# A three-phase image kernel: the order between its turns by the statistics, eight buffers for the first turn, and plain loads with VectorE's sum in the last

## The chip, the cores and the metric

One Trainium2 chip, one core. The time is the device time in microseconds of one execution of the whole program. TensorE (PE) multiplies matrices, VectorE (DVE) and ScalarE (ACT) work elementwise, GpSimd (POOL) does elementwise sums and issues some transfers, SyncE (SP) issues most transfers. Everything is float32.

## The reference

`x` is 8 images of 128 x 128 pixels and 256 channels. Two layers follow each other, each on a group-normalized copy with a residual:

```
x = x + L0(gn(x), gamma)           # v = gn(x) as (pixels, 256)
    aTa  = v^T v                   # 256 x 256, a Gram matrix over the whole image
    L0   = gamma * v softmax(aTa) + v
x = x + L1(gn(x), ...)
    x    = (x - min) / (max - min + eps)          # over the whole image
    m_k  = box sums of x over k x k, k = 2, 4, 8, 16
    alphas = slope of log m_k over log k          # per pixel and channel
    excite = sigmoid(relu(mean(alphas) w1 + b1) w2 + b2)
    sim    = cosine of log m_k and the fitted line
    L1     = sim * sigmoid(bn(alphas)) + (1 - sim) * x * excite
```

Three things are known only when a whole image has been read: the Gram matrix (and with it the mixing matrix and both group norms), the minimum and maximum of the layer's input, and `excite`.

## The kernel before

An image is cut into 16 chunks of 8 rows, a chunk into two units (two halves of 4 rows in the input, two halves of 128 channels behind it). Four stages work on four images at once, one image apart: **A** reads x and adds up the Gram matrix on TensorE (`gram_rows`, L498). **B** reads x again, turns it, multiplies it by the mixing matrix, adds the shift on VectorE and stores h to a scratch in HBM. **C** reads h back, makes the box sums (row pairs on VectorE, wider row sums t4 and t8 on GpSimd, sums over columns by band matrices on TensorE), takes logarithms and forms two arrays p and q, where the output is p + q * scale + offset; p and q go to scratch. **D** reads q, scales it (`scale_q`, L735), adds p, turns it back on TensorE (`turn_back`, L557), copies it out of PSUM (`copy_out`, L784) and stores it.

`images` (L222) runs eleven turns: turns 0, 1 and 2 fill up (A; A and B; A, B and C), turns 3 to 7 have all four stages, and turns 8, 9 and 10 drain (B, C, D; C, D; D alone). Each engine has its own program; a turn is eight pairs of chunks, and what must wait for a whole image stands between the turns, in an order written out by hand for each engine.

**Turn 0** loads x into `xa`, two buffers of 4 rows (512 KB each): SyncE loads a buffer once TensorE has used it (L266).

**Between the turns** VectorE does, in this order (L1130 to L1180): `value_range` (min and max, through a GpSimd reduction over partitions), `stats_columns` (ends with the diagonals for TensorE), `first_pairs` for both halves of the channels (the first chunk's row pairs of the next image), the squares and `norm` of stage C's last unit, `second_pairs` of half 0, `stats_logits`, `stats_step`, the last unit's `gated` product, `second_pairs` of half 1, then the means, products, moments and roots up to `stats_mix`. The `second_pairs` wait for GpSimd's first t4 sums, because the upper rows of t2 and t4 are zero pads that GpSimd clears with two memsets (L441, L442). GpSimd does `sum_p` of half 0, `first_sums` of half 0, `sum_p` of half 1, `first_sums` of half 1; `sum_p` is a DMA that adds one array to another in SBUF and waits for `tail_done`, which `gated` sets. ScalarE does the last unit's squares, then `guess_root`, then sigmoid and `invert`, then the softmax. TensorE stands still but for the small products of the statistics; its first box sum (`box` with which = 0) comes in the next turn, behind `rows1` (L684), the clearing matmuls (L606) and four rows of the Gram matrix.

**Turn 10** has stage D alone. For each unit SyncE loads q into one of four buffers, ScalarE scales it, and GpSimd adds p from HBM by an accumulating DMA:

```
def add_p(unit, at):
    pool.wait_ge(q_scaled, unit + 1)
    apart()
    g.dma_start(qd[:, at, :], p_dram[unit], accum_op=ALU.add).then_inc(sum_ready[at], 16)
```

Of the kernel before, what the change touches and what calls it, by code (L numbers as in the profile page):

```python
# [17 lines left out]
ROWS = 8  # L18
# [26 lines left out]
POOL_CONST = 10 + 1 + 2 * len(SCALES) + 2  # L45
POOL_PAIR, POOL_IMAGE = 4, 34
# [35 lines left out]
def mk_conv_preact(nc, x, gamma, w1, b1, w2, b2, bn_gamma, bn_beta, bn_mean, bn_var, out):  # L82
    with ExitStack() as ctx:
# [53 lines left out]

        def cols(at, n=2):
            return col[:, at:at + n]
# [28 lines left out]
        xa_used = sem("xa_used")  # L168
        xt_filled = sem("xt_filled")
# [64 lines left out]
        def _(sp):  # L234
# [77 lines left out]

            def turn(s, A, Bs, Cs, Ds):
                if (A or Bs):
                    loads(s, 0, 0, 0, A, Bs, False)
                if Ds:
                    for hf in range(2):
                        store_pq(32 * (s - 2) - 2 + hf, 16 * (s - 2) - 1, hf)
                    for p in pq_stored:
                        sp.wait_ge(p, 32 * CHUNKS * (s - 2))  # L320
                        apart()
                    loads(s, 0, 0, 0, False, False, True)
# [37 lines left out]
        def _(pool):  # L360
# [5 lines left out]
            g.memset(xa[:, :, :, C:C + 1], 1.0).then_inc(pool_const, 1)  # L366
            for j, value in enumerate((EPS, TINY, 1.0, GN_EPS)):
                g.memset(cst[:, j:j + 1], value).then_inc(pool_const, 1)
            g.memset(mx[:, :], -HUGE).then_inc(pool_const, 1)
            pool.wait_ge(pool_const, 10)  # L370
            made = 10
# [27 lines left out]
            def add_rows(dst, src, hf, k, gap):  # L399

                a = k * ROWS
                if k == 1:
# [10 lines left out]
            def more_row_sums(k, hf, count, pairs):  # L413

                pool.wait_ge(pool_done, own.now())
                pool.wait_ge(t_ready[2], pairs)
                add_rows(t4, t2, hf, k, 2)
                pool.wait_ge(pool_done, own.now())
                pool.wait_ge(t_ready[4], count)
                add_rows(t8, t4, hf, k, 4)  # L420
# [13 lines left out]
            def first_sums(image, hf, behind):  # L434

                if hf == 0:
                    if behind:

                        pool.wait_ge(log_ready[3], 32 * image)
                        apart()  # L440
                    g.memset(t2[:, :, ROWS - 2:ROWS, :], 0.0).then_inc(pool_done, own.one())  # L441
                    g.memset(t4[:, :, ROWS - 4:ROWS, :], 0.0).then_inc(pool_done, own.one())  # L442
                for m in range(2):
                    if m == 1:

                        pool.wait_ge(t_ready[8], 34 * image + 2 * hf + 1)
                        apart()
                    more_row_sums(1 - m, hf, 34 * image + 2 * hf + m + 1, 34 * image + 2 * m + hf + 1)

            def turn(s, A, Bs, Cs, Ds):  # L450
                image = s - 2
                def half_chunk(i, k, hf):
# [3 lines left out]
                    more_row_sums(1 - k if hf == 1 else k, 1 - hf, u + 4 + 2 * image, u + 4 + 2 * image)  # L456

                def pair(i, first, last):
                    for k in range(2):
                        for hf in range(2):  # L460
# [4 lines left out]
                            if Ds:  # L465
# [24 lines left out]
        def _(pe):  # L490
# [7 lines left out]
            def gram_rows(n, hf, half):  # L498
                if half == 0:
                    pe.wait_ge(xa_loaded[hf], 16 * (n + 1))  # L500
                for r in (2 * half, 2 * half + 1):
                    xr = xa[:, hf, r, :]
# [3 lines left out]
                if half == 1:  # L506
# [23 lines left out]
            def box(unit, k, hf, which, first):  # L530

                pe.wait_ge(t_ready[SCALES[min(which, 2)]], unit + (2 if first and which else 3) + 2 * image_of[0])
# [24 lines left out]
            def turn_back(unit, i, at, d):  # L557

                if d == 0:
# [7 lines left out]
            def half_chunk(s, i, k, hf, A, Bs, Cs, Ds, first):  # L567
# [7 lines left out]
                if Cs:  # L575
                    box(u, k, hf, 0, first)
                if Bs:
                    turn_x(nb, 2 * hf)
                if Cs:
                    box(u, k, hf, 2, first)  # L580
                    box(u, k, hf, 1, first)
                if Cs:
                    box(u, k, hf, 3, first)
# [5 lines left out]
                if Ds and not first:  # L589
                    turn_back(2 * nd + hf - 1, *behind(8 * (s - 3) + i, k, hf), 0)  # L590
# [821 lines left out]
```

## Time and profile before

| | us |
|---|---|
| median of 3 runs | 6241.43 (6239.41 to 6245.17) |
| the profiled execution | 6245.49, its span 6243.6 |
| DVE busy | 5222.7 (84% of the span) |
| PE busy | 4976.2 (80%) |
| ACT busy | 4828.5 (77%) |
| POOL busy | 1806.9 (29%) |

Row of the page: the span in 40 equal slices (156 us each), busy tenths of the engine in each slice (9 is 90% or more), and the granted TensorE clock in tenths of full speed.

```profile
PE   6968888699969998699969998799968887666632
DVE  1348999799979999799979999799989999788820
POOL 0012332233332333233323333333323332333311
PEclk9989999899989999899979999899979998788855
DMA  3544655588968988588858888589857777566678
```

How the rows further down are read. A line of the windows is: stretch in us from the start, its length, then busy us and instructions of PE, PE's weight loads, DVE, ACT and POOL, then the granted clock, the share of time that the 16 DMA engines were busy, and GB/s. A line of the waits is: engine, tile and line, what it waited for, us in total, times, longest. A line of the timeline is: start in us, us that it took, engine, line, operation, written and read tiles, shape, and how many of its kind in a row; in brackets the idle time ahead of it and what ended that. A line of the queues is: queue, packets, MB, share of the 16 engines' time. The turns end near 124, 419, 1092, 1790, 2490, 3190, 3890, 4590, 5293, 5976 and 6243 us.

### The profile page before, as it was taken

What the parts mean: (1) busy time and instruction counts of PE and PEld (TensorE: products, weight loads), DVE (VectorE), ACT (ScalarE), POOL (GpSimd) and SP (SyncE); (2) the same over time, 40 slices, a digit from 0 to 9 for tenths busy, and PEclk for the clock granted to TensorE, in tenths of its full rate; (3) what the DMA queues carried; (4) which work ended last, traced back from release to release, by engine and by line L of the source; (5) the groups of instructions that cost most, each with busy time, mean ns of one, the idle gap of its engine ahead of it and who ended that gap; (6) DMA issues with size and microseconds to landing.
All of it is one profiled execution on the core that took longest, in us unless ns stands there. A gap on an engine that the chain in (4) does not pass through costs nothing.

```text
span 6243.6 us, 108779 instructions
## 1 busy us (share of the span) xinstructions
PE 4976.2 (80%) x35320; PEld 4609.1 (74%) x35320; DVE 5222.7 (84%) x6293; ACT 4828.5 (77%) x5203; POOL 1806.9 (29%) x1361
## 2 busy tenths in 40 slices
PE   6968888699969998699969998799968887666632
PEld 5758888688858888688858887688857777566621
DVE  1348999799979999799979999799989999788820
ACT  0117888599959999599959999599959998688843
POOL 0012332233332333233323333333323332333311
PEclk9989999899989999899979999899979998788855
DMA  3544655588968988588858888589857777566678
GB/s 122 179 157 149 191 189 176 160 267 267 268 175 239 270 268 248 165 269 268 268 161 247 268 269 249 162 267 269 269 158 230 230 237 226 146 183 188 181 182 202
DMA packets 874514, 1344.68 MB, mean 215 GB/s; under 512 B 38704, under 2 KB 694096, under 8 KB 857936
## 3 DMA queue, kind: packets, MB, share of 16 engines
q1 hardware_dynamic: 800592, 1073.93, 49.1%
q0 software_dynamic: 73728, 268.47, 23.7%
q8 instruction: 85, 1.39, 0.1%
q14 instruction: 109, 0.89, 0.0%
HBM read 671.16 MB, written 536.87 MB: 193 GB/s over the span
## 4 chain that ended last, share of the span: by engine, by line
PE 36%; ACT 27%; issue 17%; DVE 10%; DMA 9%; ACTq 1%; POOL 1%; DVEq 0%; SPq 0%; POOLq 0%
PE even L545 14%; PE h_ps L526 8%; ACT logs L725 4%; ACT logs L763 4%; PE g_ps L503 4%; ACT logs L750 3%; ACT odd L725 3%; ACT logs L753 3%; DMA ut<-logs 3%; PE odd L554 3%; ACT logs L749 2%; DMA qd<-p_scratch 2%; PE o_ps L563 2%; ACT xt L712 2%; DMA hr<-h_scratch 2%
## 5 line engine op out<-in xcount | busy, mean ns | idle before, releaser
L545 PE MATMUL even<-band,t 128*128 128x128 f32 x12288 | 1871.0, 284 | 277.3 <-ACT logs L725 275.9
L545 PEld LDWEIGHTS even<-band,t 128*128 128x128 f32 x12288 | 1638.2, 199 | 330.5 <-issue 330.5
L407 POOL TENSOR_TENSOR t<-t 128x1024 f32<-128x1024 f32 (+3 forms) x800 | 1353.2, 1704 | 1034.1 <-DVE logs L1045 902.8
L526 PE MATMUL h_ps<-mix,xt 128*128 128x256 f32 x4096 | 994.1, 385 | 192.4 <-ACT xt L712 190.0
L526 PEld LDWEIGHTS h_ps<-mix,xt 128*128 128x128 f32 x4096 | 737.5, 190 | 322.4 <-ACT xt L712 242.0
L432 POOL DMA_DIRECT2D ut<-logs x256 | 224.6, 877 | 2588.4 <-DVE logs L1061 2508.4
L725 ACT ACTIVATE logs<-even,col 128x1024 f32<-128x1024 f32 x512 | 570.6, 1114 | 403.7 <-PE even L545 393.8
L547 PE MATMUL even<-band,t 128*128 128x128 f32 x4096 | 792.2, 275 | 0.0
L503 PE MATMUL g_ps<-xa 128*128 128x257 f32 x2048 | 621.9, 385 | 23.7 <-DMA xa<-in_x_dram 23.7
L563 PE MATMUL o_ps<-ident,qd 128*128 128x128 f32 x2048 | 359.2, 304 | 349.1 <-ACT o_sb L790 205.1
L930 DVE CUSTOM_DVE_ANT_0 h_out<-h_ps,shift,mx 128x512 f32<-128x512 f32 x512 | 383.0, 748 | 293.5 <-PE h_ps L526 289.6
L547 PEld LDWEIGHTS even<-band,t 128*128 128x128 f32 x4096 | 622.4, 192 | 0.0
L563 PEld LDWEIGHTS o_ps<-ident,qd 128*128 128x128 f32 x2048 | 269.6, 155 | 404.6 <-ACT o_sb L790 231.2
L545 PE MATMUL odd<-band,t 128*128 128x128 f32 x4096 | 516.0, 281 | 4.3 <-ACT ut L732 4.3
L545 PEld LDWEIGHTS odd<-band,t 128*128 128x128 f32 x4096 | 496.6, 198 | 4.6 <-issue 4.6
L712 ACT ACTIVATE xt<-xt_ps 128x512 f32<-128x512 f32 x512 | 300.3, 586 | 230.3 <-PE xt_ps L516 230.3
L504 PEld LDWEIGHTS g_ps<-xa 128*128 128x128 f32 x2048 | 390.7, 191 | 58.2
L961 DVE SCALAR_TENSOR_TENSOR t<-hr,col 128x128 f32<-128x128 f32 (+1 forms) x368 | 358.9, 975 | 73.2 <-POOL t L407 36.3
L790 ACT ACTIVATE o_sb<-o_ps 128x512 f32<-128x512 f32 x512 | 299.1, 584 | 127.6 <-PE o_ps L563 126.9
L1007 DVE TENSOR_TENSOR logs<-logs 128x1024 f32<-128x1024 f32 x256 | 388.5, 1517 | 10.4 <-DMA ut<-logs 8.2
L504 PE MATMUL g_ps<-xa 128*128 128x129 f32 x2048 | 396.0, 275 | 0.0
L739 ACT ACTIVATE qd<-qd,col 128x1024 f32<-128x1024 f32 x256 | 315.4, 1232 | 78.1 <-DMA qd<-q_scratch 56.4
(185 smaller groups left out, 10100.0 us busy)
## 6 DMA issues: line engine op xcount, KB each, us to landing
xa<-in_x_dram SPq DMA_DIRECT2D x256, 512.0 KB, 8.6
xb<-in_x_dram SPq DMA_DIRECT2D x256, 512.0 KB, 8.5
h_scratch<-h_out SPq DMA_DIRECT2D x128, 1024.0 KB, 8.7
hr<-h_scratch SPq DMA_DIRECT2D x256, 512.0 KB, 6.8
q_scratch<-logs SPq DMA_DIRECT2D x256, 512.0 KB, 4.6
ut<-logs POOLq DMA_DIRECT2D x256, 512.0 KB, 6.5
p_scratch<-ut SPq DMA_DIRECT2D x256, 512.0 KB, 2.6
qd<-q_scratch SPq DMA_DIRECT2D x256, 512.0 KB, 8.3
```

What stands on the lines that cost most here:

```text
L407: ins = g.tensor_tensor(dst[:, hf, d:d + n, :], src[:, hf, d:d + n, :], src[:, hf, e:e + n, :], ALU.add)
L503: t.matmul(g_ps[:, 0:C + 1], xr[:, 0:CH], xr[:, :], start=False, stop=False, skip_group_check=True)
L504: ins = t.matmul(g_ps[:, C + 1:C + 2 + CH], xr[:, CH:C], xr[:, CH:C + 1], start=False, stop=False, skip_group_check=True)
L526: ins = t.matmul(h_ps[:, r * C:(r + 1) * C], xt[:, q % 2, jh, r, :], mix[:, jh, :], start=(jh == 0), stop=(jh == 1))
L545: ins = t.matmul(o, src[:, hf, at, :], band[:, which, :], start=True, stop=(which < 3))
L547: ins = t.matmul(o, t8[:, hf, new + j, :], band[:, which, :], start=False, stop=True)
L563: ins = t.transpose(o_ps[:, r * CH:(r + 1) * CH], qd[:, at, (4 * d + r) * W:(4 * d + r + 1) * W], ident[:, :])
L712: a.activation(xt[:, q % 2, :, :, :].rearrange("p j r w -> p (j r w)"), xt_ps[:, :], ACT.Copy).then_inc(xt_copied, 1)
L725: a.activation(dst, src[:, :], ACT.Ln, bias=col[:, EPSR:EPSR + 1]).then_inc(log_ready[which], 1)
L930: d.tensor_tensor_reduce(h_out[:, k, 2 * q:2 * q + 2, :].rearrange("p r c -> p (r c)"), h_ps[:, :], shift[:, :, :].rearrange("p r c -> p ( ...
L961: ins = d.scalar_tensor_tensor(t2[:, hf, at:at + rows, :], hr[:, hf, at:at + rows, :], col[:, NEG2:NEG2 + 1], hr[:, hf, before:before + ro ...
L1007: d.tensor_tensor(logs[:, hf, 4, :], logs[:, hf, 0, :], logs[:, hf, 2, :], ALU.add).then_inc(dve_done, own.one())
```

## The change

**Turn 0.** `first_turn` of SyncE loads x into eight buffers in turn: the two of `xa` and six that lie in t2 and t4, which nothing uses in this turn. `first_grams` of TensorE works through them in a loop of four times eight. GpSimd writes ones into the six new buffers' last column.

**Turn 10.** `last_turn` of SyncE loads q and p of each unit with plain transfers, p into `late_p`, which lies in t8, and then stores the chunk two back. `add_p` of VectorE adds them after ScalarE has scaled q. GpSimd has nothing to do in this turn.

**Between the turns.** VectorE: `stats_columns` goes ahead of everything, `value_range` and the squares follow, then `stats_logits`, `norm`, `stats_step`, then the first row pairs of both halves in one piece, and then the last unit's product. `second_pairs` and its wait for GpSimd are gone. GpSimd: both `sum_p` come ahead of both `first_sums`; the memsets of t2 and t4 are gone, and the sums over the upper rows copy 2 rows (4 for t8) and add 6 (4) where they added 8 rows. ScalarE: `guess_root` goes ahead of the squares, the softmax ahead of `invert`. TensorE: the first box sum of the next turn goes between the moments and `rows1`.

```diff
+            def first_turn():
+
+                def eight(g, first):
+                    for j in range(8):
+                        if not first:
+                            sp.wait_ge(xa_used, 8 * g + j - 5)
+                            apart()
+                        sp.dma_start(early[j][:, :, 0:C], x_sub[8 * g + j]).then_inc(early_loaded[j], 16)
+                eight(0, True)
+                with sp.Fori(1, 4) as g:
+                    eight(g, False)
+
+            def last_turn(s):
+
+                def pair(i, first):
+                    for k in range(2):
+                        nd = 16 * (s - 3) + 2 * i + k
+                        for hf in range(2):
+                            at = 2 * k + hf
+                            sp.wait_ge(o_filled, 2 * (2 * nd + hf) + 2)
+                            apart()
+                            sp.dma_start(qd[:, at, :], q_dram[2 * nd + hf]).then_inc(q_loaded[at], 16)
+                            sp.dma_start(late_p[:, at, :], p_dram[2 * nd + hf]).then_inc(p_loaded[at], 16)
+                        if not first:
+                            store(nd - 2, k)
+
+                def store(nd, k):
+                    sp.wait_ge(o_copied, 4 * nd + 5)
+                    apart()
+                    sp.dma_start(out_chunk[nd], o_sb[:, k, :, :]).then_inc(o_stored[k], 16)
+                pair(0, True)
+                with sp.Fori(1, PAIRS) as i:
+                    pair(i, False)
+                for k in range(2):
+                    store(16 * (s - 2) - 2 + k, k)
...
-            def first_sums(image, hf, behind):
-
-                if hf == 0:
-                    if behind:
-
-                        pool.wait_ge(log_ready[3], 32 * image)
-                        apart()
-                    g.memset(t2[:, :, ROWS - 2:ROWS, :], 0.0).then_inc(pool_done, own.one())
-                    g.memset(t4[:, :, ROWS - 4:ROWS, :], 0.0).then_inc(pool_done, own.one())
+            def first_sums(image, hf):
+
                 for m in range(2):
-                    if m == 1:
-
-                        pool.wait_ge(t_ready[8], 34 * image + 2 * hf + 1)
-                        apart()
-                    more_row_sums(1 - m, hf, 34 * image + 2 * hf + m + 1, 34 * image + 2 * m + hf + 1)
...
+                if top:
+                    apart()
+                    g.tensor_copy(dst[:, hf, a:a + gap, :], src[:, hf, a:a + gap, :]).then_inc(pool_done, own.one())
+                    parts = [(a + gap, a, ROWS - gap)]
+                elif k == 1:
...
-                    sum_p(32 * (s - 1) - 2, 0)
-                if Bs:
-                    first_sums(s - 1, 0, Cs)
-                if Cs:
-                    sum_p(32 * (s - 1) - 1, 1)
-                if Bs:
-                    first_sums(s - 1, 1, False)
+                    for hf in range(2):
+                        sum_p(32 * (s - 1) - 2 + hf, hf)
+                if Bs:
+
+                    for hf in range(2):
+                        first_sums(s - 1, hf)
 
             images(lambda lo, hi: own.loop(lo, hi, POOL_IMAGE), turn)
...
+            def first_grams():
+                with pe.Fori(0, 4) as g:
+                    for j in range(8):
+                        pe.wait_ge(early_loaded[j], 16 * (g + 1))
+                        gram_of(early[j], range(SUB), True)
+
...
+                if d == 0 and alone:
+                    pe.wait_ge(p_added, unit - 2 * CHUNKS * (B - 1) + 1)
+                elif d == 0:
                     pe.wait_ge(sum_ready[at], 16 * (i + 1))
...
+                if Bs:
+
+                    box(32 * (s - 1), s - 1, 0, 0, 0, True)
+                if A:
+                    stats_rows(s)
...
                     offset(u - 1, 16 * (s - 1) - 1, 1)
+                if A:
+                    guess_root(s, var_ready, VAR, RS, rs_guess)
+                if Cs:
                     square_contrasts(u - 1, 16 * (s - 1) - 1, 1, (0, 1))
-                if A:
-                    guess_root(s, var_ready, VAR, RS, rs_guess)
-                if Cs:
                     sigmoid(u - 1, 1, (0, 1, 2))
+                if A:
+                    softmax_exp(s)
+                if Cs:
                     invert(u - 1, 1, (0, 1, 2, 3))
-                if A:
-                    softmax_exp(s)
                 if Cs:
...
+                row_pairs(1, hf, load, False)
...
+            def add_p(unit, i, at):
+                dve.wait_ge(q_scaled, unit + 1)
+                dve.wait_ge(p_loaded[at], 16 * (i + 1))
+                d.tensor_tensor(qd[:, at, :], qd[:, at, :], late_p[:, at, :], ALU.add).then_inc(p_added, 1)
...
+                if A:
+                    stats_columns(s)
...
-                if A:
-                    stats_columns(s)
-                if Bs:
-                    first_pairs(s - 1, 0)
-                    first_pairs(s - 1, 1)
                 if Cs:
                     two = two_squares(u - 1, 1)
                     add_slopes(u - 1, 1)
                     three = three_squares(u - 1, 1, two)
+                if A:
+                    stats_logits(s)
+                if Cs:
                     norm(u - 1, 1, three)
-                if Bs:
-                    second_pairs(s - 1, 0)
-                if A:
-                    stats_logits(s)
+                if A:
                     stats_step(s, Bs)
+                if Bs:
+                    for hf in range(2):
+                        first_pairs(s - 1, hf)
                 if Cs:
                     gated(u - 1, 1, product(u - 1, 1, similarity(u - 1, 1)))
-                if Bs:
-                    second_pairs(s - 1, 1)
```

## Rows read from the trace of the kernel before

**Rows 1.** Windows over turn 0, one boundary and turn 10.
```profile
10.00:124.00 114.00, 90.74 (x510) 80.06 (x510) 0.00 (x0) 0.00 (x0) 0.00 (x0) 0.99 0.45 140
2490.00:2553.00 63.00, 16.64 (x61) 14.16 (x61) 50.51 (x111) 15.92 (x23) 23.89 (x17) 0.53 0.49 151
6008.00:6243.00 235.00, 71.33 (x256) 45.84 (x256) 0.00 (x0) 73.66 (x94) 25.89 (x30) 0.50 0.82 202
```

**Rows 2.** Waits of TensorE in turn 0, 10 to 124 us.
```profile
PE g_ps L503 <- DMA xa<-in_x_dram: 23.3, 15, 1.9
```

**Rows 3.** Timeline of the boundary between turns 4 and 5.
```profile
2496.11 1.23 DVE L1061 SCALAR_TENSOR_TENSOR logs<-logs,ut 128x1024 f32<-128x1024 f32 x1
2498.09 2.39 DVE L1200 TENSOR_SCALAR col<-col 128x2 f32<-128x2 f32 x1
2499.19 1.26 POOL L442 MEMSET t<- 128x1024 f32 x1
2500.92 0.16 DVE L1271 TENSOR_SCALAR col<-col 128x2 f32<-128x2 f32 x1
2503.82 0.28 DVE L1282 TENSOR_SCALAR h_out<-ones,col 128x128 f32<-128x128 f32 x1
2529.52 1.22 DVE L1049 TENSOR_TENSOR logs<-logs 128x1024 f32<-128x1024 f32 x1
2534.67 5.23 POOL L407 TENSOR_TENSOR t<-t 128x1024 f32<-128x1024 f32 x2
2543.79 0.42 DVE L1348 TENSOR_TENSOR h_out<-h_out,o_ps 128x256 f32<-128x256 f32 x1
2550.97 2.07 PE L684 MATMUL o_ps<-h_out,ones 128*128 128x128 f32 x8 [3.38 <-DVE h_out L1369]
2562.60 2.02 PE L545 MATMUL even<-band,t 128*128 128x128 f32 x16 [0.94 <-ACT logs L725]
```

**Rows 4.** Timeline, boundary of turns 8 and 9: a small VectorE operation beside GpSimd's sums.
```profile
5331.30 5.12 POOL L407 TENSOR_TENSOR t<-t 128x256 f32<-128x256 f32 x4 [1.09 <-DVE t L961]
5335.45 0.98 DVE L1230 SCALAR_TENSOR_TENSOR col<-col,late 128x2 f32<-128x2 f32 x1
```

**Rows 5.** Timeline, boundary of turns 0 and 1: VectorE's logits and step.
```profile
134.73 0.69 DVE L1286 COPY h_out<-xt_ps 128x512 f32<-128x512 f32 x1 [2.83 <-PE h_ps L653]
144.10 0.48 DVE L1333 SCALAR_TENSOR_TENSOR h_out<-h_out,col,xt 128x256 f32<-128x256 f32 x1
```

**Rows 6.** Timeline, boundary of turns 1 and 2: one `row_pairs`.
```profile
458.51 1.53 DVE L961 SCALAR_TENSOR_TENSOR t<-hr,col 128x128 f32<-128x128 f32 x2
```

**Rows 7.** Timeline, boundary of turns 8 and 9: last `norm`, second box.
```profile
5309.39 1.23 DVE L1045 TENSOR_TENSOR logs<-logs 128x1024 f32<-128x1024 f32 x1
5339.05 3.75 PE L545 MATMUL even<-band,t 128*128 128x128 f32 x16 [2.30 <-ACT logs L725]
```

**Rows 8.** Timeline of turn 10: beginning, two output copies, last store.
```profile
5989.50 0.86 POOL L432 DMA_DIRECT2D ut<-logs  x1 [11.48 <-DVE logs L1061]
5997.27 1.77 SPq L278 DMA_DIRECT2D qd<-q_scratch  x4
6000.75 2.44 ACT L739 ACTIVATE qd<-qd,col 128x1024 f32<-128x1024 f32 x2 [9.34 <-DMA qd<-q_scratch]
6058.64 0.60 ACT L790 ACTIVATE o_sb<-o_ps 128x512 f32<-128x512 f32 x1 [4.20 <-PE o_ps L563]
6062.33 0.60 ACT L790 ACTIVATE o_sb<-o_ps 128x512 f32<-128x512 f32 x1 [0.16 <-PE o_ps L563]
6238.85 0.40 SPq L351 DMA_DIRECT2D out_dram<-o_sb  x1
```

**Rows 9.** DMA queues in turn 10, 6040 to 6230 us.
```profile
q1 hardware_dynamic: 16727, 25.98, 44.9%
q0 software_dynamic: 3698, 13.44, 39.3%
```

**Rows 10.** DMA queue of SyncE in turn 9, 5400 to 5900 us.
```profile
q1 hardware_dynamic: 49437, 65.57, 36.6%
```

More of the change, by code:

```diff
@@ L168, in mk_conv_preact @@
         xa_used = sem("xa_used")
+        early_loaded = [sem(f"early_loaded{j}") for j in range(8)]
+        p_loaded = [sem(f"p_loaded{j}") for j in range(4)]
+        p_added = sem("p_added")
         xt_filled = sem("xt_filled")
@@ L366, in _ @@
             g.memset(xa[:, :, :, C:C + 1], 1.0).then_inc(pool_const, 1)
+            for j in range(2, 8):
+                g.memset(early[j][:, :, C:C + 1], 1.0).then_inc(pool_const, 1)
             for j, value in enumerate((EPS, TINY, 1.0, GN_EPS)):
@@ L499, in gram_rows, with gram_of @@
                 if half == 0:
[L500 to L502 removed]
+                    pe.wait_ge(xa_loaded[hf], 16 * (n - CHUNKS + 1))
+                gram_of(xa[:, hf, :, :], (2 * half, 2 * half + 1), half == 1)
+            def first_grams():
[3 more added lines that the diff above has]
+                        gram_of(early[j], range(SUB), True)
+            def gram_of(x, rows, last):
+                for r in rows:
+                    xr = x[:, r, :]
                     t.matmul(g_ps[:, 0:C + 1], xr[:, 0:CH], xr[:, :], start=False, stop=False, skip_group_check=True)
@@ L505, in gram_rows @@
                                    skip_group_check=True)
-                if half == 1:
+                if last:
                     ins.then_inc(xa_used, 1)
@@ L528, in mix_x, with box @@
                 ins.then_inc(h_filled, 1)
-            def box(unit, k, hf, which, first):
-                pe.wait_ge(t_ready[SCALES[min(which, 2)]], unit + (2 if first and which else 3) + 2 * image_of[0])
+            def box(unit, image, k, hf, which, first):
+                pe.wait_ge(t_ready[SCALES[min(which, 2)]], unit + (2 if first else 3) + 2 * image)
                 if which == 0:
@@ L574, in half_chunk @@
                     gram_rows(n, hf, 0)
-                if Cs:
-                    box(u, k, hf, 0, first)
+                if Cs and not first:
+                    box(u, image_of[0], k, hf, 0, first)
                 if Bs:
@@ L589, in half_chunk @@
                 if Ds and not first:
-                    turn_back(2 * nd + hf - 1, *behind(8 * (s - 3) + i, k, hf), 0)
+                    turn_back(2 * nd + hf - 1, *behind(8 * (s - 3) + i, k, hf), 0, not Cs)
                 if A:
@@ L595, in half_chunk @@
                 if Ds and not first:
-                    turn_back(2 * nd + hf - 1, *behind(8 * (s - 3) + i, k, hf), 1)
+                    turn_back(2 * nd + hf - 1, *behind(8 * (s - 3) + i, k, hf), 1, not Cs)
             image_of = [None]
@@ L610, in pair @@
                             half_chunk(s, i, k, hf, A, Bs, Cs, Ds, first and k == 0 and hf == 0)
-                pair(0, True)
-                with pe.Fori(1, PAIRS) as i:
-                    pair(i, False)
+                if not (Bs or Ds):
+                    first_grams()
+                else:
+                    pair(0, True)
+                    with pe.Fori(1, PAIRS) as i:
+                        pair(i, False)
                 if Cs:
@@ L1069, in half_chunk @@
                 v, vf = u - 1, 1 - hf
+                if Ds and not Cs:
+                    add_p(2 * nd + hf, i, 2 * k + hf)
                 if tail:
```

55 lines of the change are left out of this document (31 added, 24 removed).

## Prediction

> **What bounds the kernel now.** I read the slices first. In most of the span VectorE is 90% busy or more; dips come at the two ends and between the turns, and the change touches only these. So I priced three stretches, with the windows, then the waits, then the timeline. In turn 0 TensorE is busy 90.7 of 114 us, and what it lacks it waited for one thing, the load of x, 23.3 us in 15 waits [rows 1, 2]. At a boundary between full turns TensorE works 16.6 of 63 us, VectorE 50.5 [rows 1]: the reader should see a chain that runs through VectorE, with one end at `rows1` (L684) and the second box sum (L545) as the point where the next turn is under way [rows 3]. In turn 10 nobody is busy, but the DMA engines are at 0.82 [rows 1]: 44.9% of their time is the plain queue with 25.98 MB, 39.3% GpSimd's accumulating queue with only 13.44 MB [rows 9]. An accumulated byte costs 1.7 times a plain one.
>
> **Turn 0.** The gain is the wait for loads: with eight buffers a load has seven units of time to land, and TensorE's own work stays. At TensorE's pace (two units, each 512 KB, in 2 x 2.65 us: 90.7 us less 5 for start and clearing, over 32) the engines must move some 200 GB/s; they moved 140 at a share of 0.45 [rows 1], so that is a share of about 0.64, and they hold. **23.3 us** saved. Six small memsets come ahead on GpSimd, below 1 us together and beside the loads of the parameters: 0, or 1 without that cover.
>
> **A boundary between full turns.** I lay the new order along the old clock [rows 3]. The last `gated` of the loop ends at 2497.3. `stats_columns` comes now at once; it took from 2500.9 to 2504.0, 3.1 us. Then the rest of what stood from 2497.3 to 2500.9, 3.6 us, of which 2.2 was one tiny operation (L1200, 2.39 us, where its like take 0.16) that ended with GpSimd's memset; that memset is gone, so 1.4: 2501.8. Two squares sums and a slope sum, 1.2 + 0.2 + 1.2 (L1049's kind): 2504.4. Logits, softmax and step: 9.85 us where GpSimd is idle [rows 5], with `norm` inside ScalarE's softmax: 2514.3. TensorE's products for the logits (3 us after the diagonals) are under the squares. Row pairs: four steps of the size of the 1.53 us for one [rows 6], 6.0: 2520.3. Three operations of 1.2 to 1.25: the last product ends at T = 2524.0. Before, they began at 2529.5 and so ended at 2533.3 [rows 3].
>
> Now GpSimd. Its wait for `tail_done` stands ahead of all its sums; queued behind it are all sixteen of its operations, and TensorE's second box waits for them. In the old trace the sums began 1.4 us behind the product (2534.67 [rows 3]). One half took 5.2 + 5.1 us [rows 3, 4]; the new upper part copies 6 of its 16 rows instead of adding them, so I estimate 9 a half, 18 for both: GpSimd is busy from T + 1.4 to T + 19.4 = 2543.4. VectorE's statistics run beside it, and the trace shows what that costs: L1200 ended at 2500.48, the memset at 2500.45 [rows 3]; a 128x2 operation with two SBUF inputs (L1230, 0.98 us) ended at 5336.43, GpSimd's four sums at 5336.42 [rows 4]. A small VectorE operation of this kind waits for the end of GpSimd's current one. The chain from the moments to the diagonals has fourteen of them, GpSimd has sixteen; so I let the chain end with GpSimd's last sum, plus 0.8: `rows1` at 2544.2 instead of 2551.0, 6.8 us earlier. The rule has a name: the Trainium skill, "SBUF — State Buffer", Who interferes with whom, says that GpSimd and VectorE share one port pair as an exclusive lock, held for the whole instruction. It speaks against putting the sums beside the statistics, and the trace agrees (2.39 against 0.16 us).
>
> TensorE's box goes under this chain: sixteen matmuls of 2.0 us, and ScalarE's logarithm behind it, for which the second box waited 0.9 [rows 3]. Its new wait, for the row pairs of half 0, is over at 2517; `rows1` stands behind it, and the diagonals come last. 2.8 us more. Nothing else is late: `scale_q` needs q on the chip, 11.3 us after `sum_p` is issued (5989.5 to 6000.75 [rows 8]), so T + 12. Together **9.5 us**. The bounds: 0 (the chain comes as late as before) and 21.5 (GpSimd costs nothing). ScalarE's `guess_root` costs its squares 0.5 us, and they are not last.
>
> There are six such boundaries, and the one between turns 1 and 2 has the same statistics: 7 x 9.5. **Boundary 8 to 9** has none. `norm` ended at 5310.6 [rows 7]; it loses 2.2 of memset and 2.8 of row pairs ahead: 5305.6, then pairs 6.0 and products 3.7, 5315.3. q is there 0.6 + 11.3 later, 5327.2, scaling and logarithm 2.3, second box at 5329.5 for 5339.05: 9.5 again, with half 0's sums done at 5326. Sum of boundaries: **76 us**.
>
> **Turn 10.** A chunk moves 3.146 MB (q, p, out). The plain queue's rate is 25.98 MB in 0.449 x 190 us, 305 GB/s [rows 9]: 10.33 us a chunk with the engines always busy, 165.3 for 16. It starts at 5997.3 with 1.8 us of latency (3.5 to q's use, less 1.7 for its bytes [rows 8]). Behind the last load come scaling and the new sum, 1.2 each, 3.7 of turning and copying (one unit apart: 6058.64 to 6062.33), and of the last store's 4.75 us to the end of the span 1.35 that are not bytes: 7.5 [rows 8]. End at 6171.9 instead of 6243.6, **71.7 us**. The sum on VectorE, 1.2 of 5.2 us a unit, is hidden under the transfers; so are TensorE and ScalarE (3.7 a unit). New waits: TensorE on `p_added`, VectorE on p, and SyncE on the copies of a chunk with the next chunk's loads behind it. Bounds: at turn 9's rate, 358 GB/s [rows 10], 8.8 a chunk, gain 96.4; at the old share of busy time, 84%, 12.3 a chunk, gain 40.2. I take the turn's own rate, since its mix of packets is nearest. The Trainium skill, "DMA: Bandwidth & Descriptors", Where 436 GB/s comes from, gives some 358 GB/s as a core's share of HBM; by it the chunk would take 8.8 us and the sum would be 6046.
>
> **Sum.** 23.3 + 76 + 71.7 = 171.0. The profiled execution took 6245.5, so 6074.5; the median of the runs lies 4.1 below it, so **6070**.
>
> **The rivals.**
> (a) Turn 10 is held by its round trips, not by bytes: four buffers, a store queued behind loads, engines 84% busy as now. For it: they never were fuller in this turn. Against: the accumulation, which put GpSimd and a second landing into each round trip, is gone. 12.3 us a chunk: 6102.
> (b) GpSimd's sums cost the chain nothing, because VectorE gets in first. Then from L1348 to `rows1` pass 7.2 us as in the old trace [rows 3], from T + 1.0: 2532.2, 12.0 earlier than my 2544.2, seven times: 5986. Against: both stalls above.
> (c) The boundaries give nothing: VectorE and GpSimd hold each other up, and the second box comes as late as before. For it: in the old order the sums were spread over the gaps. 76 more: 6146.
> (d) Turn 0 doesn't do what it says: SyncE doesn't run ahead and TensorE waits as before. 23.3 more: 6094.
> (e) Slower: in turn 10 nothing overlaps, since SyncE stands at the store's wait with the loads behind it. Loads 6.9 + 1.8, scaling, sum and two units 9.8, store 4.75: 23.3 a chunk, 372.8 against the present 246.3, 126.5 more, less the 99.3 of the other two stretches: 27.2 more than now, 6269. It decides from 21.6 us a chunk, (246.3 + 99.3) / 16. Against: four buffers are loaded ahead of that wait.
>
> **How the numbers follow.** Forecast 0.54 (own range 6040 to 6102), (a) 0.20, (b) 0.09, (c) 0.09, (d) 0.06, (e) 0.02. The range is 6010 to 6110: it holds the forecast, (a) and (d), and leaves out (b), (c) and (e), 0.20. All but (e) and a mixture near it are faster: faster by over 0.2% 0.97, within 0.2% 0.01, slower 0.02 (0.2% is about what a measurement of this kernel can tell from no change).
>
> **What would show it.** Turn 0: no wait for x, its end near 101 us instead of 124. A boundary: `stats_columns` 3.4 us earlier, GpSimd's sums in one block of about 18 us, small VectorE operations of 0.5 to 1.8 us inside it, `rows1` right behind it. If these are 0.16 us, (b) holds. Turn 10: DMA share above 0.9 with 290 to 310 GB/s; a share near 0.84 is (a). The turns' own inside must not change; if it does, the sum is wrong by what they share.

## The result, and the profile after

| | before | after |
|---|---|---|
| median, us | 6243.3 (6239.41 to 6245.38) | 5991.08 (5982.8 to 5995.84) |
| ratio | | 0.9595 [0.9581, 0.9609] |
| span of the profiled execution, us | 6243.6 | 5992.4 |

The change takes 252 us off. The forecast was 6070; the kernel is 79 us faster than that and lies below the range of 6010 to 6110. The profiled spans differ by 251.2 us.

From the page of after: busy time of the engines, then the 40 slices (150 us each), to be laid beside the slices of before.

```profile
PE 4980.4 (83%) x35320; PEld 4617.6 (77%) x35320; DVE 5203.9 (87%) x6325; ACT 4822.4 (80%) x5203; POOL 1749.3 (29%) x1351
DVE  1349999899989999899998999899998999788882
DMA  4645555689967988698877898689876787566669
```

TensorE, VectorE and ScalarE do the same work within 20 us; only idle time went. The dips of VectorE between the turns are 8 where they were 7, and the last slice has the DMA engines at 9.

Where it went, from turn to turn. Turn 0 is measured to the end of its last matmul (124.5 us in before, 96.0 in after). A boundary is measured from the first operation of `range_columns` (L1184 in before, L1254 in after), which hands the range of the image to GpSimd and is called the start of the range below, to the second box sum (L545, L601), the point at which the next turn is under way.

| stretch | predicted | measured |
|---|---|---|
| turn 0 | -23.3 | -28.5 |
| eight boundaries | -76 | -124.5 |
| inside the turns | 0 | +3.8 |
| turn 10 (first load of q to the end of the span) | -71.7 | -102.0 |

| boundary of turns | 1/2 | 2/3 | 3/4 | 4/5 | 5/6 | 6/7 | 7/8 | 8/9 |
|---|---|---|---|---|---|---|---|---|
| before, us | 58.95 | 70.93 | 74.93 | 75.38 | 75.47 | 74.64 | 70.37 | 46.21 |
| after, us | 48.72 | 55.22 | 55.67 | 55.47 | 56.17 | 55.65 | 55.49 | 40.03 |

Windows of after that answer to [rows 1], with turn 0 cut a little wider; the first line is that same stretch of before.

```profile
9.00:119.00 110.00, 86.74 (x482) 75.78 (x481) 0.76 (x6) 0.00 (x0) 0.00 (x0) 0.98 0.46 143
9.00:91.00 82.00, 82.00 (x484) 74.33 (x484) 0.77 (x6) 0.00 (x0) 0.00 (x0) 1.00 0.63 198
5850.00:5990.00 140.00, 71.25 (x256) 45.75 (x256) 39.21 (x32) 74.38 (x96) 0.00 (x0) 0.50 0.98 354
```

In turn 0 TensorE does as many matmuls in 82 us as before in 110, without a gap. In turn 10 the DMA engines are at 0.98 and move 354 GB/s; they moved 202 [rows 1].

The boundary between turns 4 and 5 in after (timeline; it answers to [rows 3]). The range starts at 2415.0 here and at 2487.2 in before, so 72.2 is to be taken off the clock of before. Rows between those shown are left out.

```profile
2450.67 1.22 DVE L1126 SCALAR_TENSOR_TENSOR logs<-logs,ut 128x1024 f32<-128x1024 f32 x1
2452.51 0.86 POOL L490 DMA_DIRECT2D ut<-logs  x1 [25.38 <-DVE logs L1126]
2453.05 0.72 POOL L458 COPY t<-t 128x256 f32<-128x256 f32 x1
2456.46 3.76 PE L601 MATMUL even<-band,t 128*128 128x128 f32 x16
2456.83 0.16 DVE L1430 TENSOR_TENSOR col<-col 128x2 f32<-128x2 f32 x1
2458.86 0.87 DVE L1309 TENSOR_SCALAR h_out<-ident,col 128x128 f32<-128x128 f32 x4
2460.01 1.70 PE L752 MATMUL o_ps<-h_out,ones 128*128 128x128 f32 x8
2460.82 1.80 POOL L465 TENSOR_TENSOR t<-t 128x768 f32<-128x768 f32 x1 [7.05 <-issue]
2465.92 1.09 ACT L793 ACTIVATE logs<-even,col 128x1024 f32<-128x1024 f32 x1
2470.25 0.39 POOL L458 COPY t<-t 128x256 f32<-128x256 f32 x1
2470.43 1.80 PE L601 MATMUL even<-band,t 128*128 128x128 f32 x11 [2.14 <-POOL t L465]
```

The last product (L1126, the T of the prediction) ends at 2451.9, GpSimd's first copy comes 1.2 us later, as forecast. But then GpSimd does nothing for 7.05 us, released by nothing that the profile shows ("issue"). In this hole VectorE's small operations run at 0.16 us, and `rows1` (L752) begins at 2460.0, before GpSimd's first real sum. The second box waits for the sums of half 0, which end at 2470.3; the logarithm (L793) was done at 2467.0.

I had overlooked the same hole in the trace of before. Two of its rows that stand in no group above, the reduction over partitions and the first sums behind it:

```profile
2494.08 0.59 POOL L476 PARTITION_ALL_REDUCE rr<-rr  x1 [17.05 <-issue]
2507.80 4.88 POOL L407 TENSOR_TENSOR t<-t 128x1024 f32<-128x1024 f32 x2 [7.35 <-DVE t L976]
```

The row of 7.35 names VectorE's row pairs as its releaser, and those of half 0 were done at 2505.5, 2.3 us before the sums; that hid the hole. The memsets of [rows 3] stand between the reduction and it, and they ran without one.

The reduction itself starts late too. VectorE hands over its last input (L1189) at 2487.84, and the reduction starts at 2494.08, 6.2 us later; at all eight boundaries of both kernels this is 5.9 to 6.3 us. It costs next to nothing here, since VectorE comes to the result later than that or waits 0.2 us for it (8/9 of after).

### The profile page after: what moved, and what is told of

It reads as the page before. It is cut to its first block and busy times, and to the rows that moved or that the text cites. A ratio compares the mean times of both kernels' runs of the same rounds, so it can differ in the third digit from the quotient of the medians.

```text
span 5992.4 us, 108675 instructions
## 1 busy us (share of the span) xinstructions
PE 4980.4 (83%) x35320; PEld 4617.6 (77%) x35320; DVE 5203.9 (87%) x6325; ACT 4822.4 (80%) x5203; POOL 1749.3 (29%) x1351
## 5 line engine op out<-in xcount | busy, mean ns | idle before, releaser
L601 PE MATMUL even<-band,t 128*128 128x128 f32 x12288 | 1886.2, 285 | 304.5 <-ACT logs L793 266.6
L601 PEld LDWEIGHTS even<-band,t 128*128 128x128 f32 x12288 | 1652.0, 200 | 358.2 <-issue 336.6
L465 POOL TENSOR_TENSOR t<-t 128x1024 f32<-128x1024 f32 (+3 forms) x800 | 1315.7, 1657 | 876.1 <-DVE logs L1110 779.6
L793 ACT ACTIVATE logs<-even,col 128x1024 f32<-128x1024 f32 x512 | 569.8, 1113 | 380.6 <-PE even L601 370.6
L559 PE MATMUL g_ps<-xa 128*128 128x257 f32 x1856 | 561.7, 384 | 0.3 <-DMA xa<-in_x_dram 0.3
L601 PE MATMUL odd<-band,t 128*128 128x128 f32 x4096 | 515.0, 280 | 0.0
L601 PEld LDWEIGHTS odd<-band,t 128*128 128x128 f32 x4096 | 496.2, 198 | 0.0
L1072 DVE TENSOR_TENSOR logs<-logs 128x1024 f32<-128x1024 f32 x256 | 397.1, 1551 | 9.6 <-DMA ut<-logs 7.1
L560 PEld LDWEIGHTS g_ps<-xa 128*128 128x128 f32 x1856 | 354.4, 191 | 52.7
L1030 DVE SCALAR_TENSOR_TENSOR t<-hr,col 128x128 f32<-128x128 f32 (+1 forms) x368 | 334.6, 909 | 43.7 <-DMA hr<-h_scratch 38.8
L1105 DVE TENSOR_TENSOR logs<-logs 128x1024 f32<-128x1024 f32 x256 | 313.7, 1225 | 59.6 <-ACT logs L821 46.2
L560 PE MATMUL g_ps<-xa 128*128 128x129 f32 x1856 | 359.8, 276 | 0.0
```

Source lines behind the costliest of these rows:

```text
L465: ins = g.tensor_tensor(dst[:, hf, d:d + n, :], src[:, hf, d:d + n, :], src[:, hf, e:e + n, :], ALU.add)
L559: t.matmul(g_ps[:, 0:C + 1], xr[:, 0:CH], xr[:, :], start=False, stop=False, skip_group_check=True)
L560: ins = t.matmul(g_ps[:, C + 1:C + 2 + CH], xr[:, CH:C], xr[:, CH:C + 1], start=False, stop=False, skip_group_check=True)
L601: ins = t.matmul(o, src[:, hf, at, :], band[:, which, :], start=True, stop=(which < 3))
L793: a.activation(dst, src[:, :], ACT.Ln, bias=col[:, EPSR:EPSR + 1]).then_inc(log_ready[which], 1)
L1030: ins = d.scalar_tensor_tensor(t2[:, hf, at:at + rows, :], hr[:, hf, at:at + rows, :], col[:, NEG2:NEG2 + 1], hr[:, hf, before:before + ro ...
```

## Experiments

Two explanations are tried. Theory R: behind the reduction over partitions GpSimd's first elementwise sum pays some 7 us in which nothing runs, and this hole keeps its sums away from VectorE's chain. Rival L: VectorE's small operations hold GpSimd out until they are through.

### The order alone, and the ends alone

order_only is the changed kernel with turns 0 and 10 as before; ends_only is the kernel before with the new turns 0 and 10.

```diff
# order_only, from the changed kernel
-                if not (Bs or Ds):
-                    first_turn()
-                    return
...
-                    if not Cs:
-                        last_turn(s)
-                        return
...
-                            if Ds and Cs:
+                            if Ds:
                                 add_p(...)
...
```

> The new order between the turns alone; turn 0 and turn 10 are as before. If the boundaries gave what the two traces differ by there (second box 10 to 20 us earlier at eight boundaries, 124 us in all), the time is 6243 - 124 = 6119, between 6110 and 6130. If my sum of 76 us was right and the rest came from the ends or from inside the turns, it is 6167.

> Turn 0 and turn 10 new, the order between the turns as before. By the two traces the ends gave 28.7 and 101.9 us: 6243 - 131 = 6112, and with order_only the two savings add up to the whole 251 within 5 us. By my sum (23.3 and 71.7) it is 6148. If the parts need each other, the savings don't add up.

Measured: order_only 6128.32 us, ratio 0.9817 [0.9801, 0.9834], 114.8 us gained; ends_only 6107.01, ratio 0.9784 [0.9767, 0.98], 136.2 us gained. Together 251.0 for a whole of 252: the parts don't touch each other. Each lies up to 9 us off what the stretches of the two traces had let expect (6119 and 6112), in opposite directions. Both savings are above the forecast's 76 and 95.0. In order_only `rows1` of boundary 4/5 comes 44.97 us behind the start of the range, as in after.

### A tiny sum that takes the hole away, and no reduction at all

```diff
# warm, from the changed kernel
 g.partition_all_reduce(rr[:, 2:4], rr[:, 0:2], 128, RMAX).then_inc(range_out, 1)
+pool.wait_ge(pool_done, own.now())
+g.tensor_tensor(spare[:, :], cst[:, 0:2], cst[:, 2:4], ALU.add).then_inc(pool_done, own.one())
...
# no_reduce, from the changed kernel
-g.partition_all_reduce(rr[:, 2:4], rr[:, 0:2], 128, RMAX).then_inc(range_out, 1)
+g.tensor_copy(rr[:, 2:4], rr[:, 0:2]).then_inc(range_out, 1)
```

> The changed kernel with one more tiny sum (128x2) on GpSimd right behind the reduction over partitions. Theory R (the first elementwise sum of GpSimd behind a reduction starts 7 us late, because GpSimd changes its code; this gap kept its sums out of VectorE's statistics): the tiny sum takes the 7 us, GpSimd's first real sum follows its copy at once, 2 us behind the last product instead of 9; small VectorE operations then last 0.5 to 1.8 us, rows1 comes 6 to 12 us later than in the changed kernel at the seven boundaries with statistics, and the kernel is 15 to 60 us slower than it, 6005 to 6050. Theory L (VectorE's stream of small operations keeps GpSimd out until it ends): the gap stays where it is and the time stays at 5991.

> The changed kernel with the reduction over partitions replaced by a plain copy on GpSimd, so the range is that of each partition alone. Theory R: no gap of 7 us ahead of GpSimd's first sum at any boundary, and the same collision with VectorE's small operations as in warm. Theory L: the gap is still there.

Measured: warm 6021.1 us, ratio 0.9644 [0.9628, 0.966]; no_reduce 6021.84 in a single run. Timeline of warm at the boundary between turns 4 and 5 (the range starts at 2425.5):

```profile
2441.10 0.77 POOL L526 TENSOR_TENSOR spare<-cst 128x2 f32<-128x2 f32 x1 [7.74 <-issue]
2463.63 0.73 POOL L459 COPY t<-t 128x256 f32<-128x256 f32 x1
2464.00 2.13 POOL L466 TENSOR_TENSOR t<-t 128x768 f32<-128x768 f32 x1
2466.87 1.28 DVE L1295 TENSOR_SCALAR gate<-gate 128x2 f32<-128x2 f32 x1
2468.86 1.72 DVE L1435 TENSOR_TENSOR col<-col 128x2 f32<-128x2 f32 x1
2476.00 4.00 DVE L1312 TENSOR_SCALAR h_out<-ident,col 128x128 f32<-128x128 f32 x4
2480.24 2.07 PE L755 MATMUL o_ps<-h_out,ones 128*128 128x128 f32 x8 [9.86 <-DVE h_out L1442]
```

The tiny sum, which has no business but to be there, takes the 7.7 us, at a place where nobody needs GpSimd. The real sums then follow their copy at once, and they meet the chain: 1.28 us for 0.16, 1.72 for 0.16, 4.00 for four that took 0.87. `rows1` comes at 54.7 instead of 45.0. So a kernel without the hole is 30 us slower. And without the reduction, at the same boundary of no_reduce, there is no hole:

```profile
2431.11 0.18 POOL L523 COPY rr<-rr 128x2 f32<-128x2 f32 x1 [10.78 <-DVE mx L1259]
2468.73 2.12 POOL L465 TENSOR_TENSOR t<-t 128x768 f32<-128x768 f32 x1
```

Theory R holds: the hole belongs to the change from the reduction to elementwise sums, a copy does not pay it (the copy at 2453.05 in after stood ahead of it), and L falls, since in both runs the sums start amid the same small operations. A reduction that lasts longer than its row says is out as well: in after the hole comes 30 us behind the reduction, with DMA issues and a copy in between. In no_reduce the copy that stands for the reduction starts 0.2 us behind VectorE's last input, where the reduction took 6 us to start: the change to the reduction has its delay too. The Trainium skill, "GPSIMD Engine Reference", Instruction dispatch, says that GpSimd's kernels can be loaded at run time and that the first call to a freshly loaded one pays some 6 us with no visible instruction. The rows agree in kind, at 6.9 to 8.1 us, which is more; that the way back to the ordinary sums costs it too is this case's to show.

### The hole closed and the sums held back

```diff
# warm_hold, from warm
                 if Bs:
+                    if A:
+                        pool.wait_ge(diag1_ready, s + 1)
+                        apart()
                     for hf in range(2):
                         first_sums(s - 1, hf)
```

> The changed kernel with two additions: the tiny GpSimd sum (128x2) right behind the reduction over partitions, as in the run named warm, and at each boundary that has group-norm statistics GpSimd's first sums wait until the new diagonals are ready (diag1_ready), so they run behind VectorE's small operations and not beside them. Theory R (the first elementwise sum behind the reduction reloads GpSimd's code for 7 us, and this gap is what kept the sums out of the chain; beside the sums every small VectorE operation waits for GpSimd's current one): rows1 comes 45 us behind the start of the value range as in the changed kernel (54.7 in warm), the sums start at once behind the wait, half 0 is done some 9.5 us later, the second box starts at 54 to 55 (55.5 in the changed kernel, 63.5 in warm); boundary 8 to 9, which has no such wait, keeps warm's 36.3 (40.0 in the changed kernel). Sum 7 x 1 + 3.7: 5980 to 5988 us. Rival: the order between VectorE and GpSimd is not what delayed warm, the tiny operation or something it moves is: then 6010 to 6025 as warm.

> The run named warm_hold once more, beside the changed kernel on the same chip, to say whether it beats it. Expected from the first look and the sum 7 x 0.3 (second box 55.2 instead of 55.5) + 3.8 (boundary 8 to 9) + the boundary of turns 1 and 2 (43.25 instead of 48.7, 5.5): 8 to 11 us under the changed kernel, ratio to the kernel before 0.957 to 0.959. Rival: the difference of 8 us was one of the places: a ratio within 0.001 of the changed kernel's.

> The changed kernel itself, beside hold_again on the same chip: 5985 to 5997 us, ratio to the kernel before 0.958 to 0.961.

Measured: 5983.44 us, ratio 0.9577 [0.9561, 0.9593], and again 5982.06, 0.9584 [0.9571, 0.9597], beside the changed kernel's 5989.96, 0.9595 [0.9582, 0.9608]. Timeline of warm_hold, same boundary (the range starts at 2413.25):

```profile
2458.20 1.16 PE L757 MATMUL o_ps<-h_out,ones 128*128 128x128 f32 x8
2458.57 0.40 POOL L459 COPY t<-t 128x256 f32<-128x256 f32 x1 [6.94 <-DVE h_out L1444]
2458.94 1.80 POOL L466 TENSOR_TENSOR t<-t 128x768 f32<-128x768 f32 x1
2468.50 2.05 PE L606 MATMUL even<-band,t 128*128 128x128 f32 x16 [0.53 <-POOL t L466]
```

`rows1` is back at 45.0. Only a wait separates this kernel from warm, and it is 38 us faster: that is what keeping the sums off the chain is worth. `rows1` comes 9.7 us earlier at each full boundary; the second box, which waits for the later sums, comes 4.2 to 8.8 us earlier at the seven boundaries with statistics and 48 in all, of which about 10 are lost again inside the turns. The second box comes at 55.25 here (55.47 in after), at 43.25 for 48.72 at boundary 1/2, and at 36.27 for 40.03 at 8/9, where the hole stood on the path of after. Both medians lie some 8 us under the changed kernel's, with intervals that overlap: likely better, not proven so.

### The hole in the old order

```diff
# warm_before: the two lines of warm in the kernel before
```

> The kernel before with the same tiny GpSimd sum behind the reduction over partitions. Theory R: the reload now lies from about 2494.7 to 2501.7 of the old clock and is over when the first row pairs are ready (2505.5), so the first sums start at 2505.5 instead of 2507.8; the second row pairs come when VectorE reaches them (2514.9) and waited for nothing. What is gained is at most 2.3 us a boundary, and it is not on the chain: 6228 to 6245, so the reload that was overlooked in the old profile cost the old order next to nothing. Rival: the old order was held by the reload, 7 us at each of 8 boundaries: near 6190.

Measured: 6230.79 us, ratio 0.998 [0.997, 0.999]; 12 us gained, inside what was expected. GpSimd's timeline, boundary 4/5 (the range starts at 2479.3):

```profile
2494.78 0.63 POOL L479 TENSOR_TENSOR spare<-cst 128x2 f32<-128x2 f32 x1 [8.06 <-issue]
2498.02 5.61 POOL L408 TENSOR_TENSOR t<-t 128x1024 f32<-128x1024 f32 x2 [0.17 <-POOL t L443]
```

The sums start at 18.8 instead of 20.6, and `rows1` comes at 61.2 instead of 63.7. I had said that nothing of this is on the chain; 2.4 to 2.6 us were at each of the boundaries 2/3 and 4/5 to 7/8, and 1.0 at 3/4. The rival, 7 us each, is out.

### Turn 10

late_accum: the changed kernel with p added again by GpSimd's accumulating DMA, SyncE's order of loads and stores kept. late_gpsimd: p loaded plainly, but from GpSimd's queue. late_no_p: no load of p.

```diff
# all three: last_turn, from the changed kernel
-                            sp.dma_start(late_p[:, at, :], p_dram[2 * nd + hf]).then_inc(p_loaded[at], 16)
...
# late_accum
-                            if Ds and Cs:
+                            if Ds:
                                 add_p(u - 32, 2 * k + hf)
...
# late_gpsimd
+                            if Ds and not Cs:
+                                pool.wait_ge(o_filled, 2 * (u - 32) + 2)
...
+                                g.dma_start(late_p[:, 2 * k + hf, :], p_dram[u - 32]).then_inc(p_loaded[2 * k + hf], 16)
```

> The changed kernel, but in turn 10 p is added again by GpSimd's accumulating DMA (VectorE's sum and the plain load of p are gone), while SyncE keeps the new order of loads and stores. Theory A (the accumulating DMA's bytes are dear, some 12 us of the DMA engines' time a chunk against 8.5): turn 10 takes 200 to 246 us instead of 144.4, the DMA share 0.82 to 0.95 at 200 to 250 GB/s, so 6050 to 6093 us. Rival B (the order of loads and stores and the number of buffers set the old turn, the accumulation does not matter): turn 10 stays near 144, 5985 to 6000 us.

> The changed kernel, but in turn 10 the plain load of p is issued by GpSimd through its own queue, where it stood before, and VectorE sums. Theory A (only the accumulation is dear): the same as the changed kernel, 5985 to 6000 us, 340 to 354 GB/s. Rival C (GpSimd's software queue is slow, whatever it carries): p's packets there take 1.5 to 1.9 times as long, turn 10 takes 190 to 246 us, 6035 to 6093 us.

> The changed kernel without the load of p in turn 10: VectorE still adds, but an old content of the buffers, so this leaves p out of the last image's output. A chunk moves 2.1 MB instead of 3.15 MB. If turn 10 of the changed kernel is bound by bytes (0.98 of the engines' time, 8.6 us a chunk), the transfers need 5.9 us a chunk and something else becomes the bound: in the old trace two output copies lay 3.7 us apart, which is 7.4 us a chunk. Then turn 10 takes 16 x 7.4 + 8 = 126 us instead of 144.4 and the kernel 5973; if TensorE and ScalarE overlap better than that, down to 16 x 5.9 + 8 = 102, 5949. The DMA share falls below 0.85 in the first case and stays above 0.95 in the second. Rival: round trips or the issue order bound turn 10, not bytes: then leaving p out changes nothing, 5985 to 5995.

| | median, us | ratio | turn 10, us |
|---|---|---|---|
| changed kernel | 5991.08 | 0.9595 [0.9581, 0.9609] | 144.3 |
| late_accum | 6096.37 | 0.9763 [0.9747, 0.9779] | 241.6 |
| late_gpsimd | 5993.3 | 0.9595 [0.9579, 0.9611] | 138.5 |
| late_no_p | 5976.64 | 0.957 [0.9556, 0.9585] | 126.7 |

The times of turn 10 are those of one trace each, and they vary from execution to execution: the changed kernel took 144.3 us and, in after_again, 141.9; warm_hold 143.2 and, as hold_again, 134.8. The DMA engines are busy all the time in the shortest too, at a higher rate (window of hold_again):

```profile
5842.00:5972.00 130.00, 71.21 (x256) 45.69 (x256) 39.22 (x32) 74.42 (x96) 0.00 (x0) 0.50 1.00 380
```

So a difference of less than 10 us in this column says nothing by itself, that of late_gpsimd among them.

Queues over 120 us of turn 10 (5860 to 5980): first the changed kernel, then late_accum (q1 is SyncE's, q0 GpSimd's), then late_gpsimd.

```profile
q1 hardware_dynamic: 22614, 44.09, 101.6%
```

```profile
q1 hardware_dynamic: 10630, 16.80, 42.7%
q0 software_dynamic: 2416, 8.78, 40.8%
```

```profile
q1 hardware_dynamic: 17983, 29.89, 66.8%
q0 software_dynamic: 4365, 15.91, 34.1%
```

On GpSimd's queue a plain load runs at 15.91 MB in 0.341 x 120 us, 389 GB/s, and the accumulating one at 8.78 MB in 0.408 x 120 us, 179 GB/s. It is the accumulation that is dear, not the queue. The kernel came out 3 us above the 6050 to 6093 expected of theory A, with nothing left for B. The order of loads and stores gave next to nothing by itself: late_accum has the new one and takes 241.6 us, before took 246.3. In it the engines are at 0.82 and TensorE waits up to 17 us for p (windows and waits of late_accum):

```profile
5850.00:6080.00 230.00, 69.09 (x248) 44.41 (x248) 0.00 (x0) 73.28 (x94) 27.72 (x32) 0.50 0.82 213
PE o_ps L618 <- DMA qd<-p_scratch: 133.5, 17, 17.2
```

Without p the turn is 17.6 us shorter (the kernel 14), at a DMA share of 0.82 (window and waits of late_no_p), so then TensorE and ScalarE hand each other the two halves of a unit, (126.7 - 7.5) / 16 = 7.4 us a chunk, as expected from [rows 8]. The changed kernel is bound by bytes, but only 0.5 to 1.1 us a chunk above that next bound, by the spread of 134.8 to 144.3 us.

```profile
5860.00:5970.00 110.00, 67.51 (x243) 43.57 (x244) 37.20 (x31) 69.92 (x91) 0.00 (x0) 0.50 0.82 273
PE o_ps L620 <- ACT o_sb L857: 37.8, 54, 0.8
```

## Why the prediction was right or wrong

**What bounds the kernel.** Right: the change moved only the three kinds of stretch, and they gave 255.0 us, of which 3.8 came back inside the turns.

**Turn 0.** The mechanism was right: no wait of the matmuls is left, and 1.2 us of their weight loads; rival (d) is out. The size was low, 23.3 for 28.5. The step that failed is "TensorE's own work stays": over the same matmuls TensorE's busy time fell from 86.74 to 82.00 us. The row of its weight loads, which I passed over, has the whole wait; the matmuls' row [rows 2] starts counting only when the last matmul has run out (waits of before, 5 to 125 us; the matmuls' own row says 23.3 over this stretch as well):

```profile
PEld g_ps L503 <- DMA xa<-in_x_dram: 27.6, 16, 2.1
```

Another part is a stretch of before in which the granted clock was at its lower level, 1.2 GHz, behind a wait of 1.9 us for x; the 0.79 over 8 us is 3.4 us of it (window of before, then of after, then of order_only):

```profile
32.00:40.00 8.00, 7.19 (x32) 6.18 (x32) 0.00 (x0) 0.00 (x0) 0.00 (x0) 0.79 0.35 110
32.00:40.00 8.00, 8.00 (x52) 7.33 (x51) 0.00 (x0) 0.00 (x0) 0.00 (x0) 1.00 0.63 203
32.00:40.00 8.00, 6.41 (x37) 5.72 (x38) 0.00 (x0) 0.00 (x0) 0.00 (x0) 1.00 0.50 149
```

That part belongs to this one execution and not to the change: order_only and warm_before load x as before did, have no such stretch in turn 0, and end it at 122.1 and 123.0 us instead of 124.5, so beside them the gain is 26 to 27. The six memsets ahead cost nothing, as said.

**A boundary: VectorE's chain up to the product.** Right. `stats_columns` came 3.3 us earlier (3.4 forecast), and the product ended 36.9 us behind the start of the range (36.8 forecast).

**GpSimd beside it.** The step that failed: "In the old trace the sums began 1.4 us behind the product", which I carried over to the new order. Those sums were the second ones behind the reduction [rows 3]; the ones that move to T + 1.4 are now the first, and pay the hole. The sums started at T + 8.9. The contention that I priced is real and a little cheaper than I put it: in warm, where the hole is gone, `rows1` comes at T + 17.8, against my T + 20.2, and the second box 63 to 64 us behind the start of the range where all four stages run. In the changed kernel the chain slipped through the hole instead, 9.7 us earlier than in warm. It did so at six boundaries. At 1/2 the hole ends too soon, and there the contention that I forecast is in the changed kernel itself (timeline of after):

```profile
422.63 1.63 DVE L1430 TENSOR_TENSOR col<-col 128x2 f32<-128x2 f32 x1
431.24 3.00 DVE L1309 TENSOR_SCALAR h_out<-ident,col 128x128 f32<-128x128 f32 x4
```

`rows1` comes 42.2 us behind the start of the range there, and 33.1 in warm_hold.

**Rival (b)** gave `rows1` at 2532.2 on the old clock, 45.0 behind the start, and it was measured at 45.04, so its number for `rows1` was right. Its 5986 for the whole, near the 5991 measured, was luck: it had 160 us for the boundaries, 35.5 more than they gave, and turns 0 and 10 gave 35.5 more than it had for them. Its reason, that VectorE gets in first, was not: take the hole away and the stalls are there, and at 1/2 they are there with it. I gave it 0.09 because both stalls in the trace spoke against it, and they did; what was missing was the question when GpSimd could start.

**The second box.** I let it come 2.8 us sooner behind `rows1` than before, held by nothing else. It is held by half 0's sums (2.14 us in the row of after above), and comes 10.4 behind `rows1` where it was 11.6. So the boundaries gave 19 to 20 us each where all four stages run, 15.7 and 14.9 at 2/3 and 7/8, 10.2 at 1/2. **At 8/9** I said 9.5 and got 6.2: there the hole lies on the path (timeline of after).

```profile
5175.17 0.72 POOL L458 COPY t<-t 128x256 f32<-128x256 f32 x1
5182.83 1.79 POOL L465 TENSOR_TENSOR t<-t 128x768 f32<-128x768 f32 x1 [6.94 <-issue]
5191.74 3.73 PE L601 MATMUL even<-band,t 128*128 128x128 f32 x16 [12.13 <-POOL t L465]
```

Half 0's sums, which I had done at T + 11, ended at T + 18; warm, where they ran at once, gained the 3.75 us. In all the boundaries gave 48.5 more than forecast. Rival (c) is out.

**Turn 10.** The mechanism was right: engines always busy, the sum on VectorE hidden, the new waits free; rivals (a) and (e) are out. The term that was mis-sized is the rate, 10.33 us a chunk. It measured (144.3 - 7.5) / 16 = 8.6 us (8.0 in the shortest execution, 134.8), and the gain was 102.0 instead of 71.7, near my bound of 96.4 at turn 9's rate [rows 10]. I took the turn's own plain rate, 305 GB/s [rows 9], "since its mix of packets is nearest"; but that rate was taken beside the accumulating transfers, which the change removes. In late_accum SyncE's plain bytes go at 16.80 MB in 0.427 x 120 us, 328 GB/s; in late_gpsimd, where the same queue carries the same transfers and only the accumulation is gone, at 29.89 in 0.668 x 120, 373; in after at 362. The smaller part, from 305 to 328, came with the new order of loads and stores. A rate that shares its engines with what is taken away is not the rate that is left. The Trainium skill's figure ("DMA: Bandwidth & Descriptors", Where 436 GB/s comes from, some 358 GB/s), which I set aside, was nearer than mine; as a limit the traces go past it, below.

**The sum.** 5.2 + 48.5 + 30.3 - 3.8 = 80 us more than the 171.0 forecast. All three terms were low, and the range, which left out (b), did not let two of them be low at once.

## What to carry to other kernels

When an operation is moved on an engine, look at what kind stands before it in the old order and in the new: a cost that belongs to a change of kind moves to whoever comes next, and the trace shows it as idle time with no releaser, or with one that had long been done. Price what is left after a change by the rate of a stretch where what is removed is absent, not by the nearest in place. Where two engines slow each other down, an explicit wait that keeps them apart can be worth more than starting at once (38 us here, against the sums let run at once), and a hole that does this by accident should be known before somebody closes it.

## What the runs showed of the hardware

- GpSimd's first elementwise sum behind a reduction over partitions begins some 7 us late (7.05, 6.94, 7.74, 8.06 in the rows above; 6.8 to 9.4 over all boundaries of all traces); copies, memsets and DMA issues in between don't. A 128x2 sum is enough to pay for it.
- The reduction over partitions starts 5.9 to 6.3 us behind its last input (before and after), where a copy in its place starts after 0.2 (no_reduce).
- A DMA that accumulates from HBM into SBUF takes the DMA engines' time at 179 GB/s where the same queue loads plainly at 389.
- The DMA engines of the one core that ran moved more than the 358 GB/s that the Trainium skill's "DMA: Bandwidth & Descriptors", Where 436 GB/s comes from, names as a core's share of HBM, with loads and stores mixed. Window over turn 10 in ends_only, then in late_gpsimd:

```profile
5970.00:6100.00 130.00, 71.35 (x256) 45.85 (x256) 39.22 (x32) 74.42 (x96) 0.00 (x0) 0.50 0.99 379
5862.00:5990.00 128.00, 69.26 (x249) 44.57 (x250) 39.20 (x32) 73.30 (x94) 15.19 (x29) 0.50 1.01 382
```

The same turn ran at 354 in the changed kernel, and took 144.3 us there and 135.8 in ends_only. Two executions of one kernel differ as much (143.2 and 134.8 us), so this is no effect of the order between the turns; what sets the rate of an execution is open.
